# Attention loop of a graph network on one Trainium2 core: the copy of the V sums out of PSUM moves from DVE to ACT, two steps behind

## The reference, cut to what matters

```
Q, K, V = x @ Wq, x @ Wk, x @ Wv
score = exp(clip(sum_d(K[src] * Q[dst]) * scale, -5, 5))     # per edge and head
wV = segment_sum(V[src] * score, dst)                         # 512 sums per node
Z  = segment_sum(score, dst)                                  # 8 sums per node
h  = wV / (Z + 1e-6)
```

## Time and profile before

| | us |
|---|---|
| median of 3 runs (3740.89 to 3746.67) | 3741.74 |
| the profiled execution, its own time | 3740.36 |
| its span, first to last instruction | 3738.0 |
| attention loop at full stream, stretch 2200 to 3400 us | 1200 |

### The profile page before, as it was taken

The page is one execution under the profiler, slowest core; times in us unless marked ns, Lnnn a source line. Parts: engine busy times, 40 slices in busy tenths (PEclk is TensorE's granted clock), DMA queues, the critical chain, the costliest instruction groups (busy, mean ns, idle before and its releaser), DMA issues. The chain is left out here.

```text
span 3738.0 us, 59649 instructions
## 1 busy us (share of the span) xinstructions
PE 3025.4 (81%) x11648; PEld 1516.3 (41%) x11649; DVE 2503.8 (67%) x4615; ACT 1632.8 (44%) x6216; POOL 1991.4 (53%) x1929
## 2 busy tenths in 40 slices
PE   4776777777777776599998999999999999999640
PEld 2332222222222222488884444444444444444210
DVE  4444333333333333555557999999999999999999
ACT  2331000000000000222226999999999999999410
POOL 1004777777777776111115555555555555555455
PEclk9887766667776767799998999999999999999865
DMA  2334666666666665344446888887888888888337
GB/s 71 110 109 133 176 176 175 177 175 180 176 175 174 176 175 153 113 143 151 147 145 245 276 277 277 278 275 270 274 276 276 276 276 277 277 276 277 104 116 218
DMA packets 263476, 750.48 MB, mean 201 GB/s; under 512 B 54179, under 2 KB 54181, under 8 KB 263402
## 3 DMA queue, kind: packets, MB, share of 16 engines
q0 software_dynamic: 197504, 615.66, 52.1%
q1 hardware_dynamic: 58910, 121.60, 10.1%
q10 hardware_dynamic: 7020, 12.80, 0.9%
HBM read 750.45 MB, written 77.83 MB: 222 GB/s over the span
## 5 line engine op out<-in xcount | busy, mean ns | idle before, releaser
L1080 POOL DMA_INDIRECT kv<-kv_d,src_t x880 | 876.9, 997 | 633.4 <-PE psw L1226 464.1
L831 POOL DMA_INDIRECT rows<-y_d,src_t x880 | 898.0, 1020 | 555.8 <-DVE rows L838 288.1
L1102 ACT ACTIVATE kv<-kv,wgt 128x64 f32<-128x64 f32 x4400 | 1096.8, 334 | 0.0
L1223 PE MATMUL psa<-kv,hot 128*128 128x512 f32 x1760 | 863.6, 613 | 29.1 <-ACT kv L1102 27.7
L921 PE MATMUL pss<-rows,hot 128*128 128x512 f16 x1760 | 632.5, 494 | 273.4 <-DMA rows<-y_d,src_t 238.0
L1132 DVE TENSOR_TENSOR kv<-kv,ps_q 128x1024 f32<-128x1024 f32 x440 | 533.0, 1211 | 32.6 <-PE ps_q L1207 24.0
L1145 DVE TENSOR_REDUCE score<-kv 128x16 f32<-128x1024 f32 x440 | 531.2, 1207 | 0.0
L1019 ACT ACTIVATE var<-var 128x512 f32<-128x512 f32 x2 | 1.3, 629 | 1187.7 <-DVE var L1006 1187.7
L1223 PEld LDWEIGHTS psa<-kv,hot 128*128 128x128 f32 x1760 | 304.1, 190 | 395.9 <-issue 387.1
L1207 PE MATMUL ps_q<-sums,hotT 128*128 x1760 | 454.4, 381 | 0.1
L855 DVE TENSOR_SCALAR rd<-psc 128x1 f32 (+1 forms) x49 | 7.7, 158 | 599.7 <-PE psc L923 599.7
(11 more groups left out here) (191 smaller groups left out, 3620.1 us busy)
## 6 DMA issues: line engine op xcount, KB each, us to landing
kv_d<-o_sb SPq DMA_DIRECT2D x49, 512.0 KB, 2.8
rows<-y_d,src_t POOLq DMA_INDIRECT x880, 3.7
kv<-kv_d,src_t POOLq DMA_INDIRECT x880, 5.3
y_d<-y SPq DMA_DIRECT2D x49, 256.0 KB, 2.0
x_d<-x_sb SPq DMA_DIRECT2D x49, 256.0 KB, 3.2
h_d<-h SPq DMA_DIRECT2D x49, 256.0 KB, 3.4
h1b<-h_d SPq DMA_DIRECT2D x49, 256.0 KB, 2.7
x1b<-x_d SPq DMA_DIRECT2D x49, 256.0 KB, 4.0
```

Source lines behind the costliest of these rows:

```text
L831: pool.indirect_dma_start(rows[:, u, g, :], None, y_d[0:N, :], bass.IndirectOffsetOnAxis(src_t[:, m:m + 1], 0), bounds_check=limit, oob_is ...
L1080: pool.indirect_dma_start(kv[:, u, g, :], None, kv_d[0:N, :], bass.IndirectOffsetOnAxis(src_t[:, m:m + 1], 0), bounds_check=limit, oob_is_ ...
L1102: last = nc.scalar.mul(v, v, wgt[:, u, g * HEADS + h:g * HEADS + h + 1])
L1223: nc.tensor.matmul(pss[:, ds(par, D)], hot[:, u, g, :].bitcast(F32), kv[:, u, g, D:2 * D], start=False, stop=(g == G - 1), skip_group_chec ...
```

## The change

ACT takes over the copy of the 512 sums of V. It does so in its own iteration s+2, behind `weigh` of s+1 and `copy_hot` of s+4; DVE's flush keeps only the sum of `psw`. A new semaphore (`taken`) counts the copies; PE loads the number of the new window and waits for the copy of the window two before (the last user of that half of `psa`) before it opens it. `win_t` lives longer, and the copy of the last window is ACT's too.

```diff
+        win_t = sb(life, "win_t", [1, TS], I16)
         early = ExitStack()
-        win_t = sb(early, "win_t", [1, TS], I16)
...
+                        def take_sums(s, i, u):
+                            if not isinstance(s, int) or s:
+                                [new] = load_values(mybir.EngineType.Activation, new_t, s, 1, 1)
+                                with act.If(new):
+                                    [at] = load_values(mybir.EngineType.Activation, col_t, s - 1, 1, (WINDOWS - 1) * WIDTH)
+                                    [par] = load_values(mybir.EngineType.Activation, par_t, s - 1, 1, D)
+                                    act.wait_ge(ps_made, s + U)
+                                    alone(act)
+                                    nc.scalar.copy(sums[:, ds(at, D)], pss[:, ds(par, D)]).then_inc(taken, 1)
+
                         def at(i, u):
                             if step := steps(i, u, -1):
                                 weigh(*step)
                             if step := steps(i, u, 2):
                                 copy_hot(*step)
+                            if step := steps(i, u, -2):
+                                take_sums(*step)
...
-                        times(act, at, -2, 1)
+                        times(act, at, -2, 2)
+                        act.wait_ge(ps_made, U + STEPS)
+                        nc.scalar.copy(window(WINDOWS - 1), pss[:, (WINDOWS - 1) % 2 * D:(WINDOWS - 1) % 2 * D + D])
...
-                        def flush(at, par):
+                        def flush(at):
                             nc.vector.tensor_reduce(sums[:, ds(at + D, HEADS)], psc[:, 0:2 * HEADS].rearrange("p (t h) -> p h t", t=2),
                                                     AX, ALU.add)
-                            nc.vector.tensor_copy(sums[:, ds(at, D)], pss[:, ds(par, D)])
...
+                        pe.sem_inc(taken, 2)
...
                             with pe.If(new):
+                                w = pe.value_load(win_t[0:1, ds(s, 1)], min_val=0, max_val=WINDOWS - 1)
+                                pe.wait_ge(taken, w + 1)
                                 nc.tensor.matmul(pss[:, ds(par, D)], zero[0:1, 0:P], zero[0:1, :], start=True, stop=False, skip_group_check=True)
```

More of the change, by code:

```diff
@@ L1042, in attend @@
                     sem("reduced"), sem("clipped"), sem("weighed"), sem("scaled_by_act"), sem("scaled_by_dve"))
-                ps_made, high = sem("ps_made1"), sem("weights_high")
+                ps_made, high, taken = sem("ps_made1"), sem("weights_high"), sem("sums_taken")
                 slots = sums[:, :].bitcast(F16)
@@ L1162, in flush_ended @@
                                     [at] = load_values(mybir.EngineType.DVE, col_t, s - 1, 1, (WINDOWS - 1) * WIDTH)
-                                    [par] = load_values(mybir.EngineType.DVE, par_t, s - 1, 1, D)
                                     dve.wait_ge(ps_made, s + U)
                                     alone(dve)
-                                    flush(at, par)
+                                    flush(at)
                         def at(i, u):
@@ L1186, in _ @@
                         dve.wait_ge(ps_made, U + STEPS)
-                        flush((WINDOWS - 1) * WIDTH, (WINDOWS - 1) % 2 * D)
+                        flush((WINDOWS - 1) * WIDTH)
                     @block.tensor
```

## The result

The changed kernel takes 3758.82 us (median of 6 runs, 3758.09 to 3761.30) against 3743.93 us of the kernel before in 6 runs: a ratio of 1.004, 95% interval 1.0027 to 1.0053. It is **slower by about 15 us**. The forecast was 3757 us, 15 us above before.

What follows compares the result with a forecast made beforehand. DVE, busy 392.76 of 400 us, sets the pace, the ring of waits behind it nearly as tight. Per window -0.60 + 0.99 - 0.06 = +0.33 us, times 48 +15.8, rounded to +15: 3757 us; 8-in-10 range 3734 to 3776.

Steps and rivals of the forecast that it cites:

- The gain: DVE's flush: the removed copy of 0.60 us comes off the path 48 times, 28.8 us in all.
- c: Moment when `clip` ends in step s+1, s being a new window's first step; PE's second product with zeros waits for it.
- ACT's string: ACT at a change of window: three loads, branch and wait before the copy, 1.55 us from L1090 to its start.
- The ring: Waits DVE, ACT, PE, DVE: a late exp moves DVE's multiply three steps on, at exp + 6.29 us.
- The loss of 0.99 us: DVE's multiply of s+5 starts at c + 11.00 where DVE alone would be there at c + 10.01, once a window.
- The ends of the loop's body: Gaps of 0.2 to 0.3 us, covered by the stall in two windows of eight: about 0.06 us a window.
- The sum: Per change of window -0.60 + 0.99 - 0.06 = +0.33 us; times 48 +15.8, taken as +15 us.
- Zeros: Parts set to cost nothing: ACT's load and branch in every step (0.25 us of cover), PE's load and waits.
- PE's part: PE's load of `win_t`, check and wait, about 0.95 us, covered by `expand` and the wait for `clip`: zero.
- Rival 1: ACT's string runs beside the ten scalings and is hidden, so only the gain stays: 3713 us; chance 0.13.
- Rival 2: A load on ACT at twice DVE's price, 0.57 us, makes every step grow: 3808 us; chance 0.05.
- Rival 3: PE's first product with zeros comes behind c, late from the load of `win_t`: up to 29 us more, 3786; chance 0.03.

Runs made afterwards that it cites:

- e2: Kernel before with DVE's copy taken out for 48 windows and put nowhere, their sums zeroed behind the loop; 3735.16 us with the zeroing, ratio 0.9988.
- e4: Kernel before (DVE copies) with only the load of `new_t` and the branch added on ACT in every step; 3740.41 us, ratio 1.0000.
- e5: Kernel before with PE's load of `win_t`, its check and a wait on `taken` that is already satisfied; 3740.13 us, ratio 0.9998.
- e1: Changed kernel with ACT's loads and copy of the sums of V put ahead of `copy_hot`; 3711.93 us, ratio 0.9928.
- e3: Changed kernel with ACT's copy shrunk from 512 to 64 columns, the other sums zeroed behind the loop; 3760.56 us with the zeroing, ratio 1.0053.

## Why the prediction was right, point by point

- **The gain.** 0.60 us a window at c, forecast and measured (3.99 to 3.39 us from the multiply of s+1 to the clip's end). e2 puts the removal at 30 us, with the idle time ahead of its zeroing counted to the zeroing (25 without it); the sum had 28.8.
- **ACT's string.** Forecast 1.55 us from L1090 to the copy, by DVE's row of the same string; measured 1.5, with loads of 0.26 where 0.29 was taken. Copy 0.48 forecast, 0.49 measured. Exp of s+2 at c + 4.71 forecast, c + 4.65 measured.
- **The ring.** Exp to total 2.99 forecast, 2.98 measured; total to multiply 3.30, the same. The multiply of s+5 at c + 11.00 forecast, c + 10.93 measured. The loss of 0.99 us was set a little high: it is 0.89, with 0.07 from the earlier exp and 0.03 from DVE's own arrival, c + 10.04 for c + 10.01. Of it 0.26 shows at s+4, most of that where `scale` waits for the exp (2626.55, 1.34 us behind its multiply where 1.13 is the rule).
- **The ends of the loop's body.** Their gaps fell from 7.2 to 4.8 us in the stretch, 0.06 us for each of 39 windows, as set: the eleven windows in which DVE's end falls between s+3 and s+5 lose it in the wait.
- **The sum.** +0.33 us a window forecast, +0.30 measured on average; that it is so close is in part small errors that cancel. Up to the multiply of s+3 a change gains 0.59 us (0.62 in e2; the difference is PE's late product in five changes), where 0.60 was set. At s+4 and s+5 it loses 0.84, with the ends of the body in it, where 0.93 was set. Another 0.05 comes behind s+5, nearly all at s+7, where the prediction had the loss paid for good; what it is stays open. ACT's step when it is behind was read too long as well: it takes 3.01 us (2626.30 to the next exp at 2629.31), not 3.11.
- **Zeros.** The plain step stays at 3.22 to 3.23 us, and e4 bounds the load in every step at 0.1%. PE's part was set to zero and is not quite: about 1.3 us, from the five changes shown under e5.
- **The rivals.** Rival 1 describes what the change would have been with the string beside the scalings, 28.8 us below before; e1, which has the copy ahead of `copy_hot` as well, is 27.9 below. That it isn't what the change does was read from one row, L1090's, and this held. Rival 2 needed a load at twice DVE's price; it takes 264 ns. Rival 3's sign, a first product with zeros behind c, was seen in five changes of 39, at 0.2 us each and not at the 0.6 it allowed.
- **The rule that spoke the other way.** The Trainium skill (Perfetto Trace Analysis, Optimizing Scalar/DVE Operations) says that a saturated DVE may be relieved by Scalar. The copy is indeed cheaper on ACT (0.49 us for 0.60), and e1 shows the rule's gain; the changed kernel shows that the gain is lost where the loads for the instruction's addresses stand behind a wait, and the engine idles through them for longer than the instruction takes.

## What to carry to other kernels

Work that moves to an engine with room is priced not by its duration but by where it stands in that engine's order and by what it makes late: follow the late instruction around the ring of waits to the engine that sets the pace. Instructions with addresses from registers bring a string of loads (here 0.4 us each). In this kernel it cost nothing ahead of a wait that the sequencer would sit in anyway, and its whole length behind it, less the half microsecond by which the exp may be late. When a move loses, try the order before giving it up: two parts swapped turned +0.4% into -0.7%. And test a rival in the place where it would bite: e5 added PE's load with 0.9 us of cover, and the changed kernel has 0.3.

## What was not expected

- The same load of a register takes 264 ns on ACT and 283 to 288 on PE and DVE.
- A DVE memset of 128x24576 behind the loop had 5.1 us idle ahead of it, and one of 128x21504 had 4.4, with the releaser "issue", where the copy of the last window before had none. Idle time and row together are 25.61 and 22.41 us, and both are 1.042 ns for each of the 24576 and 21504 elements; four memsets of 128x2048 in the kernel before (L1119) start 2.14 us apart, again 1.04 ns for an element, with rows of 1.76 us. So the idle time is best read as a part of the memset that its row leaves out, and it is right to subtract both in e2 and e3. Why the row begins late stays open.
